# Query and key projected once a sequence for all heads, with a masked query for each group of heads, and two changes of order on TensorE

## The reference

```python
qkv = x @ W_attn + b_attn
q, k, v = jnp.split(qkv, 3, axis=-1)          # H = 16 heads, D = C // H = 8
q = q.reshape(B, T, H, D).transpose(0, 2, 1, 3)   # k and v in the same way
att = jnp.einsum('bhtd,bhsd->bhts', q, k) * (1.0 / math.sqrt(D))
att = att + rel_bias
att = jnp.where(causal, att, -jnp.inf)
att = jax.nn.softmax(att, axis=-1)
y = jnp.einsum('bhts,bhsd->bhtd', att, v)
y = y.transpose(0, 2, 1, 3).reshape(B, T, C)
return y @ W_proj + b_proj
```

## Time and profile before

| | us |
|---|---|
| median of three runs | 1414.88 (1412.97 to 7027.12) |
| the profiled execution | 1413.66 |
| its span in the trace | 1411.9 |
| stage 1 in the trace, up to attention's first VectorE instruction | 0 to 65.26 |
| attention, up to the second ffn's first VectorE instruction | 65.26 to 379.7 |
| everything behind it | 379.7 to 1411.9 |

### The profile page before, as it was taken

One profiled execution on the slowest core, in us unless ns is written; L12 is line 12 of the kernel. 1 busy time (PEld: TensorE's weight loads), 2 busy tenths in 40 slices (PEclk: granted clock), 3 DMA queues, 4 the chain that ended last, 5 costly groups with the idle time before them and its releaser, 6 DMA issues. The chain is left out here.

```text
span 1411.9 us, 35632 instructions
## 1 busy us (share of the span) xinstructions
PE 1304.2 (92%) x10556; PEld 1112.9 (79%) x10556; DVE 956.2 (68%) x4070; ACT 784.9 (56%) x1886; POOL 780.8 (55%) x1027
## 2 busy tenths in 40 slices
PE   7789999999786879999968999999999979999998
PEld 5567777777584668888857999999988867888887
DVE  5557777776595855565637877888878848556564
ACT  2267778777436424444425666676667644444443
POOL 2068777777434265555424566655678562444453
PEclk9989999999877989999989999999999989999999
DMA  5199930000113011222112222112122102222211
GB/s 154 38 273 272 271 102 0 0 0 2 52 59 112 22 61 30 31 30 29 26 21 58 50 53 50 50 46 50 48 60 56 45 24 66 51 28 31 31 29 16
DMA packets 102600, 85.68 MB, mean 61 GB/s; under 512 B 10503, under 2 KB 90089, under 8 KB 102202
## 3 DMA queue, kind: packets, MB, share of 16 engines
q1 hardware_dynamic: 83796, 65.90, 16.9%
q0 software_dynamic: 17280, 16.17, 6.5%
q10 hardware_dynamic: 1382, 1.83, 0.5%
HBM read 21.32 MB, written 45.78 MB: 48 GB/s over the span
## 5 line engine op out<-in xcount | busy, mean ns | idle before, releaser
L1990 POOL TENSOR_TENSOR attn_z<-attn_top,attn_z 128x256 f32<-128x256 f32 x256 | 156.0, 613 | 65.7 <-DVE attn_top L1937 63.8
L1937 DVE CUSTOM_DVE_ANT_0 attn_z<-banks,rel_bias 128x128 f32<-128x128 f32 (+1 forms) x512 | 149.6, 352 | 36.8 <-PE banks L2085 35.6
L2430 POOL TENSOR_TENSOR ret_rotated<-ret_twins 128x512 f32<-128x512 f32 x64 | 82.1, 1282 | 134.6 <-DVE ret_twins L2340 134.4
L2493 ACT ACTIVATE ret_normed<-banks,ret_head_shift,ret_head_rstd 128x128 f32<-128x128 f32 x256 | 96.3, 458 | 47.3 <-DVE ret_head_shift L2364 47.0
L2023 ACT ACTIVATE attn_prob<-banks 128x384 f32<-128x384 f32 x256 | 118.8, 491 | 6.7 <-PE banks L2095 1.9
L1011 DVE SCALAR_TENSOR_TENSOR moe_block_act<-banks,moe_block_weights,moe_block_gated 128x128 f32<-128x128 f32 x276 | 77.7, 344 | 64.2 <-ACT moe_block_gated L1066 39.4
L1556 DVE SCALAR_TENSOR_TENSOR moe_block_act<-banks,moe_block_weights,moe_block_gated 128x128 f32<-128x128 f32 x276 | 77.9, 344 | 63.1 <-ACT moe_block_gated L1650 38.8
L2095 PE MATMUL banks<-ident,attn_z 128*128 128x128 f32 x768 | 108.6, 277 | 1.0 <-ACT attn_prob L2023 0.7
L2095 PEld LDWEIGHTS banks<-ident,attn_z 128*128 128x128 f32 x768 | 84.0, 140 | 14.6 <-issue 14.4
L2525 PE MATMUL banks<-ret_x_hi,ret_hi 128*128 128x256 f32 x256 | 85.1, 333 | 1.9 <-ACT ret_gate L2486 1.0
L1603 POOL DMA_INDIRECT out<-moe_block_y,moe_taken x37 | 58.5, 1580 | 48.5 <-ACT moe_block_y L1660 41.1
(11 more groups left out here) (366 smaller groups left out, 4256.7 us busy)
## 6 DMA issues: line engine op xcount, KB each, us to landing
slots<-moe_pad SPq DMA_DIRECT2D x12, 2560.0 KB, 23.4
ret_twins<-ret_twins SPq DMA_DIRECT2D x256, 64.0 KB, 2.0
moe_stage<-in_moe_w SPq DMA_DIRECT2D x4, 576.0 KB, 5.7
bias_reversed<-scratch SPq DMA_DIRECT2D x1, 2048.0 KB, 9.7
y_rows<-moe_pad SPq DMA_DIRECT2D x1, 2048.0 KB, 8.8
back_of_seq<-y_rows SPq DMA_DIRECT2D x16, 128.0 KB, 2.3
out<-x_res SPq DMA_DIRECT2D x8, 256.0 KB, 2.3
ret_stage<-in_ret_w SPq DMA_DIRECT2D x16, 96.0 KB, 2.1
```

What stands on the lines that cost most here:

```text
L1937: last = dve.tensor_tensor_reduce(out=z[:, s, cols], in0=ps_s[:, i, cols], in1=bias, scale=1.0, scalar=-3.0e38, op0=ALU.add, op1=ALU.max, ...
L1990: pool.tensor_tensor(z[:, s, P:WIDTH], top[:, s, 1:2].to_broadcast([P, WIDTH - P]), z[:, s, P:WIDTH], ALU.subtract).then_inc(shifted1, 1)
L2430: pool.tensor_tensor(rotated[:, k % 2], twins[:, k % 2, 0], twins[:, k % 2, 1], ALU.add).then_inc(rotated_ready, 1)
L2493: last = act.activation(normed[:, r, i, :], ps_o[:, r, i * RET_V:(i + 1) * RET_V], ACT.Identity, bias=head_shift[:, r, i:i + 1], scale=hea ...
```

## The change

q and k of all 16 heads are projected once a sequence: two float32 matmuls of 256 columns with the plain weights (128 columns for q, 128 for k, the heads interleaved so that rows 32i to 32i+31 hold four heads, one of each quad). DVE copies both out of PSUM (`copy_qk`: q plain, k with bias). For each quad ACT makes one 128x256 `q_group` out of `q_all`, with a scale and a bias that are zero in the rows of the other quads' heads; `scores` then multiplies 32 rows as before. The float32r splits of x and of the weights go, on ACT and on POOL. The jobs once a sequence stand between two pairs of `transpose_z` on PE, `attend` directly behind `scores`, and the lists of DVE, ACT and POOL are reordered. In stage 1 the flip stands ahead of the router. Nine small loads take the place of seven; the weight of q and k is 128 KB in place of 512.

```diff
@@ Opening.copy_flipped (split_qk is removed, and POOL's call of it)
-            act.mul(self.attn["q_bias"], self.attn["q_bias"], HEAD_D ** -0.5)
-            act.copy(flat(self.attn["qk_hi"]), flat(self.attn["qk_w"])).then_inc(self.qk_hi_done, 1)
+            act.mul(self.attn["q_bias"][:, :], self.attn["q_bias"][:, :], HEAD_D ** -0.5)
@@ stage 1, PE
             every_step(-4, GROUPS, U, [
-                (3, transpose_x), (1, transpose_om), (3, router_and_mid), (1, project)] + in_step(lambda n: opening.flip(pe, n), 0, FLIPS))
+                (3, transpose_x), (1, transpose_om)] + in_step(lambda n: opening.flip(pe, n), 0, FLIPS) + [(3, router_and_mid), (1, project)])
@@ attention, DVE
+            def copy_qk(it, k):
+                p = k // HEAD_GROUPS % GU
+                dve.wait_ge(qk_projected, seq(it, k))
+                wait_free(dve, scores_ready, (it * GU + k // HEAD_GROUPS - 1) * HEAD_GROUPS)
+                dve.tensor_copy(q_all[:, p, :], ps_job[:, 0, :])
+                dve.tensor_scalar(k_all[:, p, :], ps_job[:, 1, :], w["k_bias"][:, 0:1], None, ALU.add).then_inc(qk_copied, 1)
...
-                (2, divide), (11, per_seq(0, layernorm)), (5, of_head(0, bias_and_max)), (5, of_head(1, bias_and_max)),
-                (1, per_seq(LAST, residual)), (8, per_seq(0, add_v_bias)), (10, per_seq(0, normalise)),
-                (5, of_head(2, bias_and_max)), (5, of_head(3, bias_and_max))])
+                (5, of_head(0, bias_and_max)), (5, of_head(1, bias_and_max)), (5, of_head(2, bias_and_max)), (5, of_head(3, bias_and_max)),
+                (3, divide), (8, per_seq(0, add_v_bias)), (7, per_seq(0, copy_qk)), (1, per_seq(LAST, residual)),
+                (14, per_seq(0, layernorm)), (13, per_seq(0, normalise))])
@@ attention, POOL
-                pool.tensor_tensor(x_lo[:, p, :], xnT[:, p, :], x_hi[:, p, :].bitcast(F32), ALU.subtract).then_inc(x_split, 1)
...
-                (4, of_head(2, shift)), (4, of_head(3, shift)), (8, per_seq(0, split_x)), (5, of_head(0, shift)),
-                (5, of_head(1, shift)), (11, per_seq(0, inverse_std))])
+                (5, of_head(0, shift)), (5, of_head(1, shift)), (5, of_head(2, shift)), (5, of_head(3, shift)),
+                (8, per_seq(0, add_out_bias)), (14, per_seq(0, inverse_std))])
@@ attention, ACT
-                act.copy(x_hi[:, p, :], ps_x).then_inc(x_hi_ready, 1)
-                act.wait_ge(qk_projected, quad(it, k))
+            def take_group(it, k):
+
+                hg = k % HEAD_GROUPS
+                act.wait_ge(qk_copied, seq(it, k))
                 wait_free(act, scores_ready, quad(it, k, 2))
-                act.activation(qk[:, r, 0, :], ps_job[:, 0, :], ACT.Identity, bias=w["q_bias"][:, hg:hg + 1], scale=SCALE)
-                act.activation(qk[:, r, 1, :], ps_job[:, 1, :], ACT.Identity, bias=w["k_bias"][:, hg:hg + 1]).then_inc(qk_copied, 1)
+                act.activation(q_group[:, k % 2, :], q_all[:, k // HEAD_GROUPS % GU, :], ACT.Identity,
+                               bias=w["q_bias"][:, hg:hg + 1], scale=w["q_scale"][:, hg:hg + 1]).then_inc(group_ready, 1)
...
-                (3, of_head(3, exponent)), (4, of_head(2, shift_tile0)), (9, per_seq(0, copy_xT)), (2, per_seq(LAST, copy_yT)),
-                (3, copy_avT), (4, of_head(0, exponent)), (4, of_head(1, exponent)), (7, copy_qk), (4, of_head(2, exponent)),
-                (5, of_head(0, shift_tile0))])
+                (4, of_head(0, shift_tile0)), (4, of_head(2, shift_tile0)), (6, take_group), (3, copy_avT),
+                (4, of_head(0, exponent)), (4, of_head(1, exponent)), (9, per_seq(0, copy_xT)), (2, per_seq(LAST, copy_yT)),
+                (4, of_head(2, exponent)), (4, of_head(3, exponent))])
@@ attention, PE
             def project_qk(it, k):
-                p, hg = k // HEAD_GROUPS % GU, k % HEAD_GROUPS
-                wait_free(pe, qk_copied, quad(it, k, 1))
...
+                pe.wait_ge(v_ready, seq(it, k))
+                wait_free(pe, yT_ready, seq(it, k, 2))
                 for i in range(2):
-                    w_hi, w_lo = w["qk_hi"][:, i, hg, :], w["qk_lo"][:, i, hg, :]
-                    pe.matmul(ps_job[:, i, :], w_hi, x_hi[:, p, :], start=True, stop=False)
-                    pe.matmul(ps_job[:, i, :], w_hi, x_lo[:, p, :], start=False, stop=False)
-                    last = pe.matmul(ps_job[:, i, :], w_lo, x_hi[:, p, :], start=False, stop=True)
+                    last = pe.matmul(ps_job[:, i, :], w["qk_w"][:, i, :], xnT[:, k // HEAD_GROUPS % GU, :], start=True, stop=True)
                 last.then_inc(qk_projected, 1)
...
-                (5, scores), (1, per_seq(LAST, project_out)), (2, per_seq(LAST, transpose_y)), (9, per_seq(0, transpose_x)), (8, per_seq(0, project_v)),
-                (3, attend), (4, of_head(0, transpose_z)), (4, of_head(1, transpose_z)), (7, project_qk),
-                (4, of_head(2, transpose_z)), (4, of_head(3, transpose_z)), (3, transpose_heads)])
+                (5, scores), (3, attend), (4, of_head(0, transpose_z)), (4, of_head(1, transpose_z)),
+                (1, per_seq(LAST, project_out)), (2, per_seq(LAST, transpose_y)), (9, per_seq(0, transpose_x)), (8, per_seq(0, project_v)),
+                (3, transpose_heads), (4, of_head(2, transpose_z)), (4, of_head(3, transpose_z)), (7, per_seq(0, project_qk))])
@@ loads
-ATTENTION_LOADS = ("qk_w", "v_w", "proj_w", "qk_bias", "v_bias", "proj_bias", "flip")
+ATTENTION_LOADS = ("qk_w", "v_w", "proj_w", "q_bias", "k_bias", "q_scale", "v_bias", "proj_bias", "flip")
```

More of the change, by code:

```diff
@@ L90, in __init__ @@
         self.distances_ready, self.half_set, self.lora_scaled = (new_sem(nc, used, n) for n in ("distances_ready", "half_set", "lora_scaled"))
-        self.qk_hi_done, self.flipped, self.flip_copied = (new_sem(nc, used, n) for n in ("qk_hi_done", "flipped", "flip_copied"))
+        self.flipped, self.flip_copied = (new_sem(nc, used, n) for n in ("flipped", "flip_copied"))
     def load_x(self, sync):
@@ L295, in _ @@
             every_step(-4, GROUPS, U, [
-                (4, inverse_std)] + beside(pool, 1) + in_step(lambda n: opening.split_qk(pool), 1, 1))
+                (4, inverse_std)] + beside(pool, 1))
         @block.tensor
@@ L1807, in attention_phase @@
     Z, PR = 8, 8
-    SCALE = HEAD_D ** -0.5
     with ExitStack() as ctx:
@@ L1823, in attention_phase @@
         xnT = sb("xnT", [P, GU, T])
-        x_hi, x_lo = sb("x_hi", [P, GU, T], F32R), sb("x_lo", [P, GU, T], F32R)
         v_aug = sb("v_aug", [P, GU, BATCH_TILES, HEADS, 32])
-        qk = sb("qk", [P, 2, 2, T])
+        q_all, k_all = sb("q_all", [P, GU, T]), sb("k_all", [P, GU, T])
+        q_group = sb("q_group", [P, 2, T])
         z = sb("z", [P, Z, WIDTH])
@@ L2043, in transpose_x @@
                 pe.wait_ge(xn_ready, seq(it, k))
-                wait_free(pe, qk_copied, (it * GU + k // HEAD_GROUPS) * HEAD_GROUPS - 2)
+                wait_free(pe, qk_copied, seq(it, k, 1))
+                wait_free(pe, x_updated, seq(it, k, 3))
                 for j in range(BATCH_TILES):
@@ L2050, in project_v @@
                 p = k // HEAD_GROUPS % GU
-                pe.wait_ge(x_hi_ready, seq(it, k))
-                wait_free(pe, qk_copied, (it * GU + k // HEAD_GROUPS) * HEAD_GROUPS - 1)
+                pe.wait_ge(xnT_ready, seq(it, k))
                 for j in range(BATCH_TILES):
@@ L2057, in project_qk @@
             def project_qk(it, k):
-                p, hg = k // HEAD_GROUPS % GU, k % HEAD_GROUPS
-                wait_free(pe, qk_copied, quad(it, k, 1))
-                if hg == 0:
-                    pe.wait_ge(x_split, seq(it, k))
-                    pe.wait_ge(v_ready, seq(it, k))
-                    wait_free(pe, yT_ready, seq(it, k, 2))
-                elif hg == 1:
-                    wait_free(pe, x_updated, seq(it, k, 2))
-                elif hg == 2:
-                    wait_ahead(pe, x_hi_ready, seq(it, k, -1), BATCHES)
-                else:
-                    wait_ahead(pe, v_ready, seq(it, k, -1), BATCHES)
+                pe.wait_ge(v_ready, seq(it, k))
+                wait_free(pe, yT_ready, seq(it, k, 2))
                 for i in range(2):
-                    w_hi, w_lo = w["qk_hi"][:, i, hg, :], w["qk_lo"][:, i, hg, :]
-                    pe.matmul(ps_job[:, i, :], w_hi, x_hi[:, p, :], start=True, stop=False)
-                    pe.matmul(ps_job[:, i, :], w_hi, x_lo[:, p, :], start=False, stop=False)
-                    last = pe.matmul(ps_job[:, i, :], w_lo, x_hi[:, p, :], start=False, stop=True)
+                    last = pe.matmul(ps_job[:, i, :], w["qk_w"][:, i, :], xnT[:, k // HEAD_GROUPS % GU, :], start=True, stop=True)
                 last.then_inc(qk_projected, 1)
@@ L2078, in scores @@
                 rows = [slice(32 * i, 32 * i + 32) for i in range(4)]
-                q, kk = qk[:, k % 2, 0, :], qk[:, k % 2, 1, :]
-                pe.wait_ge(qk_copied, quad(it, k))
```

(18 more changed lines are left out.)

23 lines of the change are left out of this document (6 added, 17 removed).

## The result

The changed kernel takes 1362.9 us (median of four runs, 1358.9 to 1371.1) against 1413.9 (median of four): ratio 0.9667 with a 95% interval of [0.9638, 0.9696]. The ratio is estimated without the one slow run of the kernel before (7027 us), and it is not the quotient of the two medians, 0.9639. A second comparison, later and with five runs of the changed kernel, gives 1362.7 against 1408.2: 0.9675 [0.9654, 0.9696]. The forecast was 1368, a ratio of 0.968. Faster, and by the forecast's amount.

What follows compares the result with a forecast made beforehand. PE was taken to bound attention, busy 39.87 of 40 us. From 1413.66 us, attention's -40.7 and stage 1's -5.1 gave 1367.9, predicted as 1368, with a range from 1358 to 1386.

Steps and rivals of the forecast that it cites:

- The new projection at 0.94: Attention on PE, once a sequence: two float32 matmuls of 256 columns, 0.86 us, with the change-over 0.94.
- The step with y and the projection at 4.56: Attention step on PE with two transposes and the projection of q and k: 3.62 + 0.94 = 4.56 us.
- The step with x at 3.62: Attention step on PE with two transposes: 3.46 us, plus 0.16 lost waiting for head 0's exponent, 3.62.
- The attention's sum, -40.7: Attention, 62 quads at 3.93 us: 243.9 against 284.58, -40.7; filling and draining at 0, between -2 and +2.
- Stage 1, -5.1: Stage 1: the flip fills PE's waits, 3.4 us, and 1.7 more at the end; bounds 0 and -6.
- DVE near 90% and ACT and POOL at 0.8 to 0.9: Attention: DVE's work 14.0 of 15.7 us a sequence; ACT and POOL about 0.8 to 0.9 busy.
- Attend waits for the fourth exponent: Rival, attention: if ACT runs late, attend stalls 0.3 us in 47 steps, +15, 1382 us; chance 0.20.
- DVE loses its slack: Rival, attention: normalise grows by 0.6 beside POOL, scores 0.4 us late once a sequence, +6.4, 1374; chance 0.08.
- The loop turns serial: Rival, attention's softmax loop: bias waits for DVE's other work, 4.78 us a step, 1420 us; chance 0.03.
- The clock: Rival, attention: the clock falls to 1.2 GHz, about 1600 us; chance 0.02.
- The flip gains nothing: Rival, stage 1: DVE or the table limits it, 1373 us; chance 0.06.
- PE meshes better: Rival, attention: no change-overs and no exponent wait, 15.2 us a sequence, 1359 us; chance 0.06.

Runs made afterwards that it cites:

- experiment 4: Changed kernel with each of the two float32 projection matmuls issued twice: 1417.0 us, 0.9802 of the kernel before.
- experiment 6: Changed kernel with the transposes of x and of y each done twice: 1368.3 us, 0.9695 of the kernel before.
- experiment 5: Changed kernel with layernorm's statistics one quad earlier, ahead of the copies of q and k: 0.9686 of before, repeated 0.9681; with a copy added before the residual: 0.9720.
- the attention alone: Changed kernel with stage 1's flip put back behind project: 1367.4 us against 1406.9 for the kernel before, 0.9725.
- the flip alone: Kernel before with only stage 1's flip moved ahead of the router: 1401.6 us, 0.9963 of the kernel before.
- experiment 1: Two runs, the attention alone and the flip alone: 0.9725 and 0.9963 of the kernel before.
- an added copy: Changed kernel with one more 128x256 copy out of PSUM on DVE, ahead of the copies of q and k: 1401.0 us, 0.9702 of the kernel before.
- the order alone: Kernel before with only PE's list in the changed kernel's order, old projection kept in every step: 1469.8 us, 1.0465 of the kernel before.
- the jobs behind scores: Changed kernel with the jobs once a sequence put back between scores and attend: 1400.9 us, 0.9939 of the kernel before.
- experiments 2 and 3: Two runs, the order alone and the jobs behind scores: 1.0465 and 0.9939 of the kernel before, quads 344.6 and 276.8 us.

## Why the prediction was right, point by point

**PE bounds the attention before and after.** Busy 39.87 and 39.89 of 40 us. Right.

**The new projection at 0.94.** Two float32 matmuls of 256 columns at 0.86: right, since doubled they take 0.86 more (experiment 4), and the weight loads add nothing, as the forecast took it from the earlier trace rows. The 0.96 in the trace is not the same sum as the 0.94, though. It runs to the next scores and so holds the 0.10 of the change to scores, which the forecast counted elsewhere; the 0.08 for the change from transposes to the projection does not appear (0.65 from heads 2 and 3 to it in experiment 6).

**Steps of 3.78 with v or the output.** 3.78 and 3.78, to the hundredth.

**The step with y and the projection at 4.56.** 4.57 to 4.60, and this agreement is in part luck: the change-over of 0.08 that was not there and the second wait of 0.08 that was not forecast cancel. In the step with x, which has no projection, they can't.

**The step with x at 3.62.** This is the term that was mis-sized: 3.76 and 3.86 by turns. Read at 212.66: 0.87, 0.78 and 1.22 are as forecast (the 1.22 as a whole; experiment 6 shows that less of it is waiting); the last part, heads 2 and 3 to scores, takes 0.99 where 0.74 was set. 0.08 of the 0.25 is a second wait of the same kind: the forecast let head 2 wait for head 0's exponent, but not head 3 for head 1's, and the group lasts 0.90 instead of the 0.82 that it has where nothing waits (211.91), or where the wait is filled (experiment 6). About 0.05 is DVE being late with its fourth head, by experiment 5: the forecast had the bias 0.10 late and called it exactly PE's own step, and it is just over. The remaining 0.12 comes in every second sequence, at the end of the loop's body, which is two sequences (`GU = 2`; DVE, ACT and POOL branch back at 216.5 to 216.8, right where this step ends). The kernel before has a difference of the same size (18.36 and 18.51), though it shows in its step with y (4.62 for 4.42), two steps behind the loop's end; that the loop is the cause in both was not tested. If it is, the difference cancels between the kernels; the forecast drew its new sequence from single steps and left it out, while 4.59 a quad of the earlier trace rows holds it. That is 8 x 0.15 = 1.2 us.

**The attention's sum, -40.7.** Measured -36.0 in the profiled pair and -37.4 in the two later profiles for the same quads; -39.5 in time with the attention alone. The step with x gives 15.5 x 0.19 = 2.9 of the missing, the lower clock in the first quads some 1 to 2 in the profiled one. The gap between quads and whole is filling and draining: attention's whole length fell by 37.5 to 38.9, so these gained 1.5, inside the -2 to +2.

**Stage 1, -5.1.** -5.3 by the flip alone. By the trace, from where both kernels run at full rate, a step fell from 5.09 to 4.42 and the stretch by 5.4. The loads and SyncE's two issues showed nothing, as counted: with the new loads and the old flip the attention starts at 61.7, with the old loads at 61.8 (experiment 1).

**DVE near 90% and ACT and POOL at 0.8 to 0.9.** DVE 33.9 to 35.4 of 40 us (85 to 89%) in the four stretches from 140 to 300 us, ACT 33.4 to 33.6, POOL 34.1 to 35.0. The new activation was set at 0.47 and takes 0.59, inside its bounds and hidden; at ten a stretch that is 1.2 us more of ACT in 40.

**The rivals.** *Attend waits for the fourth exponent*: no; attend follows scores by 0.87, which is scores alone. *DVE loses its slack*: only at the one place named, by 0.05, not 0.4. *The loop turns serial*: no; the copies waited, as it says, but 0.29 of DVE's idle time was left behind them, and an added copy was free. Among the kernels run, the order alone is what a slower outcome looks like, mostly from another cause than the rivals': neighbours on one bank. *The clock*: 1.00 through the attention's middle. *The flip gains nothing*: -5.3 excludes it; by the interval of its ratio it is -3.5 to -7.0. *PE meshes better*: no.

**Why 1362.9 and not 1368.** Ratio for ratio the forecast (0.9677) lies inside both intervals, and the second comparison's -45.5 us meets the forecast's -45.8, where a sum 3.3 us too large in the quads is partly made up by one 1.5 too small at the stage's ends; the rest, 1 to 2 us, is below what the runs can tell. The profiled pair differs by 9 us more than that, in stages without a changed instruction and at the start. Busy time at the retention's end, in before and after, at about the same place of the stage:

```profile
1140.00:1165.00 25.00, 18.52 (x99) 15.71 (x98) 8.28 (x28) 12.05 (x28) 17.97 (x23) 0.80 0.11 35
```

```profile
1085.00:1110.00 25.00, 17.77 (x133) 15.59 (x132) 10.95 (x42) 14.30 (x34) 17.07 (x22) 1.00 0.08 27
```

In this execution of before the mean granted clock is 0.80 there, that is, 10 of the 25 us at the lower level, with 99 matmuls done where after does 133; its retention takes 419.6 us against 414.7. The flip alone has 0.80 at the same place and 418.4, the order alone, with the old projection, 415.6; the jobs behind scores, with the new one, 418.2, and the doubled transposes, also with it, 417.6. So the old or new attention does not decide it. That it goes with the execution and not with the kernel is not shown for this stage, since only the changed kernel was profiled twice and had 414.7 and 414.8. The medians speak for it: stage 1 and the attention alone account for 44 of their 45.5 us. For the start (experiment 1) and the second ffn (54.7 and 57.2 us in two profiles of one kernel) it is shown. What starts such a spell was not settled.

## What to carry to other kernels

Write out the bound engine's whole step from starts in the trace, for every kind of step, and let each wait appear as a distance between two starts: that gave three of four kinds within 0.04 us, one of them with two errors that cancel, where the two halves of experiments 2 and 3 taken singly would have given -8 and +60 us. A job once a sequence is worth placing where the bound engine waits, here between the transposes whose bank an exponent must empty (28 to 30 us for the four jobs, over half of it such waits), but not beside another user of its PSUM bank. A busy share does not show waits of 0.1 us inside a run of matmuls; doubling a piece of work that costs nothing does. And the time of stages without a changed instruction has to be taken out before a profiled pair is read: here it was 9 of 55 us.

## What the runs showed of the hardware

An activation of 128x256 float32 takes 0.59 us from on-chip memory to on-chip memory, and 0.47 from PSUM; the first also takes its scale from a column, one value a row, and which of the two makes the 0.12 was not tried. Four more float32 records of 256 columns with four full-width weight loads add 0.86 us, the loads nothing. Executions of one kernel differ by how long TensorE runs at its lower level: the doubled transposes ran in 1362.3 to 1374.1 us, and the slowest of them shows a mean granted clock of 0.953 where the fastest has 0.962. Worked out from these means, the slowest lost 12.8 us more of full-rate time (0.047 x 1372 against 0.038 x 1361), and it took 11.8 us more. In experiment 2 two neighbours on one PSUM bank cost PE 0.7 to 0.8 us each time, which is the wait until the first result was copied out.
